# Attention with a residual on one core: plain fp32 projections in place of three products of rounded parts

## What is computed

```python
q = _split_heads(jnp.einsum('bfe,ed->bfd', x, W_query))
k = _split_heads(jnp.einsum('bfe,ed->bfd', x, W_key))
v = _split_heads(jnp.einsum('bfe,ed->bfd', x, W_value))
scores = jnp.einsum('hbqd,hbkd->hbqk', q, k)
attn = jax.nn.softmax(scores, axis=-1)
out = jnp.einsum('hbqk,hbkd->hbqd', attn, v)
out = out.transpose(1, 2, 0, 3).reshape(x.shape[0], x.shape[1], HEADS * ATT_D)
out = out + jnp.einsum('bfe,ed->bfd', x, W_res)
return jax.nn.relu(out)
```

## Time and profile before

| | |
|---|---|
| median of 3 runs | 1513.08 us (1512.99 to 1513.62) |
| span of the profiled execution | 1511.5 us, 1.6 below the median |
| PE busy | 1493.2 us, 99% |
| DVE busy | 1392.5 us, 92% |
| ACT busy | 1243.9 us, 82% |
| POOL busy | 873.1 us, 58% |
| HBM | read 67.37 MB, written 67.11 MB: 89 GB/s over the span |

### The profile page before, as it was taken

One profiled execution on the slowest core, in us unless ns is written; L12 is line 12 of the kernel. 1 busy time (PEld: TensorE's weight loads), 2 busy tenths in 40 slices (PEclk: granted clock), 3 DMA queues, 4 the chain that ended last, 5 costly groups with the idle time before them and its releaser, 6 DMA issues.

```text
span 1511.5 us, 77760 instructions
## 1 busy us (share of the span) xinstructions
PE 1493.2 (99%) x32768; PEld 1404.9 (93%) x32768; DVE 1392.5 (92%) x1793; ACT 1243.9 (82%) x2050; POOL 873.1 (58%) x1548
## 2 busy tenths in 40 slices
PE   7999999999999999999999999999999999999997
PEld 6999999999999999999999999999999999999997
DVE  6999999999999999999999999999999999999996
ACT  5888888888888888888888888888888888888886
POOL 3555555555555555555555555555555555555555
PEclk9999999999999999999999999999999999999999
DMA  3444444444444444444444444444444444444443
GB/s 59 97 85 96 85 96 86 96 86 95 86 96 86 96 86 96 86 96 86 96 86 96 86 96 86 95 86 96 86 96 85 96 85 96 85 96 85 96 86 77
DMA packets 677306, 135.40 MB, mean 90 GB/s; under 512 B 545888, under 2 KB 677216, under 8 KB 677216
## 3 DMA queue, kind: packets, MB, share of 16 engines
q1 hardware_dynamic: 675840, 134.30, 42.8%
q10 hardware_dynamic: 1376, 0.26, 0.1%
HBM read 67.37 MB, written 67.11 MB: 89 GB/s over the span
## 4 chain that ended last, share of the span: by engine, by line
PE 98%; issue 0%; POOL 0%; DVE 0%; ACTq 0%; DMA 0%; ACT 0%; POOLq 0%
PE ps_so L241 18%; PE ps_pt L232 17%; PE ps_so L221 14%; PE ps_qk L199 8%; PE ps_qk L197 8%; PE ps_vr L210 8%; PE ps_qk L198 8%; PE ps_vr L211 8%; PE ps_vr L212 8%; POOL y L155 0%; DMA w_raw<-in_L_rec_W_res_dram 0%; ACTq L339 0%; POOL v_diag L168 0%; DVE row_max L369 0%; ACTq L336 0%
## 5 line engine op out<-in xcount | busy, mean ns | idle before, releaser
L155 POOL TENSOR_TENSOR y<-attn,vr 128x256 f32<-128x256 f32 x512 | 387.8, 778 | 530.8 <-DVE attn L384 509.2
L168 POOL COPY v_diag<-vr 64x264 f32<-64x264 f32 x1024 | 479.0, 468 | 103.4 <-ACT vr L298 55.8
L311 ACT COPY probs_t<-ps_pt 128x512 f32<-128x512 f32 x512 | 301.8, 589 | 157.2 <-PE ps_pt L232 157.2
L369 DVE TENSOR_REDUCE row_max<-ps_so 128x16 f32<-128x1024 f32 x256 | 313.6, 1225 | 67.8 <-PE ps_so L221 67.6
L291 ACT COPY qk<-ps_qk 128x512 f32<-128x512 f32 x512 | 301.1, 588 | 61.6 <-PE ps_qk L199 9.2
L197 PE MATMUL ps_qk<-x_hi,w_hi 128*128 128x256 f32 x1024 | 331.2, 323 | 10.3 <-DVE x_lo L360 9.5
L298 ACT COPY vr<-ps_vr 128x512 f32<-128x512 f32 x512 | 298.1, 582 | 34.0 <-PE ps_vr L212 0.7
L232 PE MATMUL ps_pt<-ident,probs 128*128 128x128 f32 x2048 | 321.4, 279 | 0.7 <-ACT probs_t L311 0.7
L374 DVE TENSOR_TENSOR shifted<-ps_so,row_max 128x1024 f32<-128x1024 f32 x256 | 313.4, 1224 | 8.8
L241 PE MATMUL ps_so<-v_diag,probs_t 128*64 128x66 f32 x8192 | 296.2, 224 | 1.4 <-DVE attn L384 0.7
L199 PE MATMUL ps_qk<-x_lo,w_hi 128*128 128x256 f32 x1024 | 291.7, 285 | 0.0
(11 more groups left out here) (21 smaller groups left out, 1690.4 us busy)
## 6 DMA issues: line engine op xcount, KB each, us to landing
x_in<-in_r_x_dram SPq DMA_DIRECT2D x1024, 64.0 KB, 2.2
out_dram<-y SPq DMA_DIRECT2D x256, 256.0 KB, 2.5
w_raw<-in_L_rec_W_query_dram ACTq DMA_DIRECT2D x1, 64.0 KB, 2.2
w_raw<-in_L_rec_W_key_dram ACTq DMA_DIRECT2D x1, 64.0 KB, 2.5
w_raw<-in_L_rec_W_value_dram ACTq DMA_DIRECT2D x2, 32.0 KB, 2.7
w_raw<-in_L_rec_W_res_dram ACTq DMA_DIRECT2D x2, 32.0 KB, 2.6
```

The costliest lines, as they stand in the source:

```text
L155: nc.gpsimd.tensor_tensor(y[:, n % 2, a * HALF:(a + 1) * HALF].rearrange("k t (p j d) -> k j (t p) d", j=2, d=D), attn[:, n % 2, a * HALF: ...
L168: nc.gpsimd.tensor_copy(v_diag[n % 2][j * F:(j + 1) * F, seq, :, :, :, j].rearrange("k a t p d -> k a (t p) d"), vr[n][seq * F:(seq + 1) * ...
L369: nc.vector.reduce_max(row_max[:, :].rearrange("q (h u) -> q h u", h=HEADS), scores, AX_X).then_inc(max_ready, 1)
```

## The change

The weights stay as they are loaded, in one tile `w`. `split_x` becomes `transpose_x`: one transposition from `x_in` straight into `x_t`, which is now the ring of four. Each group of three products becomes one product of the fp32 operands. Where TensorE waited for `xlo_ready` it waits for `xt_done`; where it waited for `wlo_ready` at the start it waits for the six DMAs of the weights. The order of the work on every engine stays.

```diff
-        w_raw = sb("w_raw", [P, 4, COLS])
-        w_hi = sb("w_hi", [P, 4, COLS], F32R)
-        w_lo = sb("w_lo", [P, 4, COLS], F32R)
+        w = sb("w", [P, 4, COLS])
...
-        x_t = sb("x_t", [P, TOK])
-        x_hi = [sb(f"x_hi{n}", [P, TOK], F32R) for n in range(RING)]
-        x_lo = [sb(f"x_lo{n}", [P, TOK], F32R) for n in range(RING)]
+        x_t = [sb(f"x_t{n}", [P, TOK]) for n in range(RING)]
...
             def project_qk(i, n, a):
-                pe.wait_ge(xlo_ready, i + 1)
+                pe.wait_ge(xt_done, i + 1)
...
-                for w in range(2):
-                    ps = ps_qk[:, w * HTOK:(w + 1) * HTOK]
-                    nc.tensor.matmul(ps, w_hi[:, w, :], x_hi[n][:, tok], start=True, stop=False)
-                    nc.tensor.matmul(ps, w_lo[:, w, :], x_hi[n][:, tok], start=False, stop=False)
-                    last = nc.tensor.matmul(ps, w_hi[:, w, :], x_lo[n][:, tok], start=False, stop=True)
+                for m in range(2):
+                    last = nc.tensor.matmul(ps_qk[:, m * HTOK:(m + 1) * HTOK], w[:, m, :], x_t[n][:, tok],
+                                            start=True, stop=True)
...
-                w_vr_hi = w_hi[:, 2:4, :].rearrange("p w c -> p (w c)")
-                w_vr_lo = w_lo[:, 2:4, :].rearrange("p w c -> p (w c)")
+                w_vr = w[:, 2:4, :].rearrange("p w c -> p (w c)")
                 for t in range(HALF):
-                    ps = ps_vr[:, t * 2 * COLS:(t + 1) * 2 * COLS]
                     tok = slice((a * HALF + t) * P, (a * HALF + t + 1) * P)
-                    nc.tensor.matmul(ps, x_hi[n][:, tok], w_vr_hi, start=True, stop=False)
-                    nc.tensor.matmul(ps, x_hi[n][:, tok], w_vr_lo, start=False, stop=False)
-                    last = nc.tensor.matmul(ps, x_lo[n][:, tok], w_vr_hi, start=False, stop=True)
+                    last = nc.tensor.matmul(ps_vr[:, t * 2 * COLS:(t + 1) * 2 * COLS], x_t[n][:, tok], w_vr,
+                                            start=True, stop=True)
...
             pe.wait_ge(ident_ready, 1)
-            pe.wait_ge(wlo_ready, 1)
+            pe.wait_ge(w_loaded, 96)
...
-            act.wait_ge(w_loaded, 96)
-            nc.scalar.copy(w_hi[:, :, :], w_raw[:, :, :]).then_inc(whi_ready, 1)
...
-            def split_x(i, n):
+            def transpose_x(i, n):
                 dve.wait_ge(x_loaded[n % 2], dma_count(i, n, 4))
-                if has(i - 1):
-                    dve.wait_ge(xlo_ready, i)
-                nc.vector.transpose(x_t[:, :], x_in[:, n % 2]).then_inc(xt_done, 1)
-                dve.wait_ge(xt_done, i + 1)
                 if has(i - 4):
                     dve.wait_ge(vr_done, halves(i - 4, 1))
-                nc.vector.tensor_copy(x_hi[n][:, :], x_t[:, :]).then_inc(xhi_ready, 1)
-                dve.wait_ge(xhi_ready, i + 1)
-                nc.vector.tensor_tensor(x_lo[n][:, :], x_t[:, :], x_hi[n][:, :].bitcast(F32),
-                                        ALU.subtract).then_inc(xlo_ready, 1)
+                nc.vector.transpose(x_t[n][:, :], x_in[:, n % 2]).then_inc(xt_done, 1)
...
-            dve.wait_ge(whi_ready, 1)
-            nc.vector.tensor_tensor(w_lo[:, :, :], w_raw[:, :, :], w_hi[:, :, :].bitcast(F32),
-                                    ALU.subtract).then_inc(wlo_ready, 1)
```

More of the change, by code:

```diff
@@ L6 @@
 F32 = mybir.dt.float32
-F32R = mybir.dt.float32r
 ALU = mybir.AluOpType
@@ L84, in attention_program @@
         ones_ready, diag_zero = sem("ones_ready"), sem("diag_zero")
-        whi_ready, wlo_ready = sem("whi_ready"), sem("wlo_ready")
-        xt_done, xhi_ready, xlo_ready = sem("xt_done"), sem("xhi_ready"), sem("xlo_ready")
+        xt_done = sem("xt_done")
         s_done, max_ready, shifted_ready, probs_ready = sem("s_done"), sem("max_ready"), sem("shifted_ready"), sem("probs_ready")
@@ L333, in step @@
                     copy_vr(i, n, 1)
-            for w, weight in enumerate((w_query, w_key)):
-                act.dma_start(w_raw[:, w, :], weight).then_inc(w_loaded, 16)
-            for w, weight in ((2, w_value), (3, w_res)):
+            for m, weight in enumerate((w_query, w_key)):
+                act.dma_start(w[:, m, :], weight).then_inc(w_loaded, 16)
+            for m, weight in ((2, w_value), (3, w_res)):
                 for j in range(2):
-                    act.dma_start(w_raw[:, w, j * F:(j + 1) * F].rearrange("e (p d) -> e p d", p=PAIRS),
+                    act.dma_start(w[:, m, j * F:(j + 1) * F].rearrange("e (p d) -> e p d", p=PAIRS),
                                   weight.rearrange("e (p j d) -> e j p d", p=PAIRS, j=2)[:, j]).then_inc(w_loaded, 16)
-            act.wait_ge(w_loaded, 96)
-            nc.scalar.copy(w_hi[:, :, :], w_raw[:, :, :]).then_inc(whi_ready, 1)
             act.wait_ge(ones_ready, 1)
@@ L388, in step @@
                 if has(i + 2):
-                    split_x(i + 2, (n + 2) % RING)
-            dve.wait_ge(whi_ready, 1)
-            nc.vector.tensor_tensor(w_lo[:, :, :], w_raw[:, :, :], w_hi[:, :, :].bitcast(F32),
-                                    ALU.subtract).then_inc(wlo_ready, 1)
-            split_x(0, 0)
-            split_x(1, 1)
+                    transpose_x(i + 2, (n + 2) % RING)
+            transpose_x(0, 0)
+            transpose_x(1, 1)
             run(step)
```

## The result

The changed kernel takes 1662.26 us (median of 4 runs, 1661.85 to 1663.13) against 1513.35 us for the kernel before on the same chip: ratio 1.0985, 95% interval 1.0972 to 1.0998. It is 9.9% slower where 3.6% faster was forecast, and it came out nearest to rival 2 in its second form (.427 us a product: 6.35 us a step, 1649 us). The profiled execution has a span of 1660.2 us.

The account below looks back on a forecast made before the run. TensorE bounds the kernel at 5.812 us a step; a ring of waits at 5.62 would take over. 253 steps' gain of 48.6 us plus 5.7 at the start gives 54.3 less: 1459 us, range 1434 to 1479 plus a microsecond above.

Parts of the forecast that it names:

- rival 2: Projections: a plain product costs four passes, .48 us (1756 us in all) or .427 (1649 us), so slower; chance 8%.
- the price of the plain product: TensorE's projections: .217 us per plain product of 256 columns, taken from the transposition's .85 ns a column.
- The removed 2.88 us: TensorE, per step: the 24 rounded projection products at .12 us each go away.
- The added 1.74: TensorE, per step: 8 plain projection products at .217 us each come in, 1.74 us.
- TensorE's sum 4.67: TensorE's own work per step falls from 5.81 to 4.67 us.
- the price decides above .36: Projections: no gain is left only if a plain product costs more than .36 us.
- Bounds .12 and .48 a product: Projections: a plain product costs at least .12 us, today's product, and at most .48, four passes at today's price.
- VectorE's split as worthless: VectorE: removing the cast and subtraction, 1.51 us a step, brings nothing to the path.
- The ring of 5.62: Scores, row_max to attn, wait of .14, next scores, weighing: this loop of waits sets each step at 5.62 us.
- The start: Before the steady state: first product at about 7.1 us, cheaper first pieces and two first steps, together -5.7 us.
- Rival 3: TensorE idles, its clock falls to the lower level, its work doubles: 9.3 us a step, some 2400 us; chance 3%.
- The signs of being wrong: Trace: a piece's two plain products over .34 us apart, another wait before first scores, or a period below 5.4.

Follow-up runs that it names:

- e3: The changed kernel with each plain product of 256 moving columns cut into two of 128, all work kept: 1691.19 us, one run.
- e6: The kernel before with all 24 rounded products but no subtraction for x_lo, the third product reading x_hi instead: 1512.42 us, ratio .9993.
- e5: The kernel before without the eight products with w_lo, x still split in full: 1458.78 us, ratio .9640.
- e1: The kernel before with one rounded product (w_hi with x_hi) in place of three, and no x_lo: 1458.33 us, ratio .9635.

## Why the prediction was wrong

**The step that failed** is the price of the plain product: "I take .217, by the row that is nearest in shape". The runs show .434, twice that, and so 8 x .434 = 3.47 us added a step where 1.74 were put in. Two readings of rows lie under it. One is this sentence: "a weighing product has 66 columns and 64 of the array's columns, two side by side, so 32 of them are 16 fillings of the array in 1.08 us, .0675 us each". The rows say x32 a step, but `weigh_values` has four loops of two, 16 products a step; in the groups that is x8192 against 16 x 256 = 4096. The 32 records are 16 products, 8 fillings, .135 us each, 2.05 ns a column. At that, 256 columns take .52 us, which alone is above the .36 where the change stops paying. The description of the kernel ahead of the prediction carries the same slip: it says 64 score products and 32 weighing products a step, where the loops make 32 and 16 (and 64 and 32 are the records). Both numbers could be checked without the chip, by multiplying the ranges of the loops.

The other row, the transposition, was counted rightly (8 a step, x2048) and was the wrong relative: it is one record of .108 us where a plain product of its shape is two of .111 (e3). I named the doubt myself ("transpositions may be served in a way of their own") and still took its .217, with the miscounted row to back it. Two wrong readings agreed with each other, .85 and 1.02 ns a column, and that agreement took the rule's chance down to 8%.

**The rule of the Trainium skill** (page "FP8 and Floating Point Precision", section "TensorE Precision Notes"), that true FP32 takes four passes, agrees with this trace in the time: 256 columns, .434 us, against .12 for a rounded product, a factor of 3.6. The trace has two records for such a product, not four, and doesn't show what lies in each. The objection that four passes at 2.4 GHz would need .110 us a filling was an objection to a count that was wrong; a filling takes .135.

**Point by point.** The removed 2.88 us: right. The added 1.74: wrong, it is 3.47. TensorE's sum 4.67: it is 6.40. That the price decides above .36: right, and .434 is above. Bounds .12 and .48 a product: they held, but the range was taken from the latency of a wait that never came to matter. VectorE's split as worthless: right (e6, e5). The ring of 5.62 with .14 for the latency: right wherever TensorE is quick, 5.60 in e1 with a latency of .10 in most steps. That e1 at 1458.33 us lands on the forecast's 1459 is in part luck. From its first row_max to its last it saved 54.8 us where 48.6 were forecast, and its start and end together gave .2 where 5.7 were forecast: 2.35 us gained before the first row_max, 2.2 lost behind the last.

The start: the first product at 7.01 was right. But of the 3.2 us that were to be gained by the first scores (2.4 + .8), .3 came. The table load of 1.28 us used to lie beside the DMAs, ahead of a cast that the change removes, and a plain piece there is four records of .43, 1.7 us and 2.08 with its last result, where I had put .86. Of the 2.5 us of the two first steps nothing was left: their distances went from 5.28 and 5.90 us to 4.83 and 6.49. The end: right, 14.4 us behind the last row_max as before. The half speed of the first products, which I called the lower of the clock's two levels, was read from their distance; the granted clock in the trace reads 1.00 in that stretch, before and after.

Rival 3, a falling clock: in e1 TensorE idles .88 us a step, its granted clock is 1.00 from 100 to 1400 us, and the weighing's 32 records still take 1.16 us. The signs of being wrong were the right ones: the two products of a piece start .43 apart, above the .34, and each line has 2048 records where x1024 was said. The chances of the three outcomes don't follow from those of the rivals: slower is 8 + 3 = 11%, not 10, and same 1.5%, not 3.

## What to carry to other kernels

Before a row of the trace becomes a price, multiply out the loops that issue it and compare with its count: a factor of two there is a factor of two in the price. A plain fp32 product cost .434 us for 256 columns and three rounded ones .36. So the three, which leave out only the product of the two lower parts, were the cheaper way here, as long as the engine that makes the parts has time. And look for the ring that comes next: here any gain on the projections would have stopped at 5.60 us a step.

## What the runs showed of the hardware

- A plain fp32 product leaves two records in the trace, a rounded one, a bf16 one and an fp32 transposition one each. From start to start, 256 columns: .434 us plain, .12 rounded; 128 columns: .223 plain, .108 for a transposition.
- 16 weighing products took 1.08 us in fp32 and .38 us in bf16.
- At the start the four records of two plain products took 2.08 us (from 7.01) where they took 1.03 later, half the speed; in the kernel before, rounded products started .21 us apart there and .12 later. The row of the granted clock reads full speed for that stretch all the same (columns: busy us and count of each engine, PEclk, DMA share, GB/s; kernel after):

```profile
7.00:9.10 2.10, 2.08 (x4) 1.18 (x4) 0.71 (x1) 0.00 (x0) 0.00 (x0) 1.00 0.72 115
```
